# The Householder steps of a graph kernel: one TensorE visit per step instead of two, with the next row formed on VectorE

## The reference

```
h = relu(layernorm(x)); x = x + L0(h)   # normalised adj, two linear layers, each with a batch norm over all tokens
h = relu(layernorm(x)); x = x + L1(h)   # two products with adj, then LSTMs over windows of 1, 2, 3 and 4 nodes
h = relu(layernorm(x)); x = x + L2(h)   # U relu(U^T h W1 + b1) W2 + b2, U = eigenvectors of a Laplacian of adj
h = relu(layernorm(x)); x = x + L3(h)   # three graph convolutions with adj * adj
```

## Time and profile before

| | us |
|---|---|
| three runs, median (lowest to highest) | 1082.08 (1081.61 to 1082.16) |
| the profiled execution | 1077.69 |
| its span in the trace | 1075.9 |
| PE busy | 942.6 |
| DVE busy | 593.2 |
| ACT busy | 529.3 |
| POOL busy | 335.7 |

### The profile page before, as it was taken

How to read it: one execution, slowest core, us unless ns; L and a number is a source line. 1 busy time by engine, 2 the same in 40 slices (tenths; PEclk the granted TensorE clock), 3 DMA queues, 4 the chain that set the end, 5 groups by cost and what they waited for, 6 DMA issues and landing times.

```text
span 1075.9 us, 12192 instructions
## 1 busy us (share of the span) xinstructions
PE 942.6 (88%) x3721; PEld 573.0 (53%) x3721; DVE 593.2 (55%) x2897; ACT 529.3 (49%) x962; POOL 335.7 (31%) x404
## 2 busy tenths in 40 slices
PE   2787485589989999899898999995899999999998
PEld 1444232544546544456344553553675865866856
DVE  5899766767634785347999198965410501503101
ACT  1566364475453654536546365441646445445531
POOL 1333100036544265441665527653210200300000
PEclk9989798699999999999998999997799999999999
DMA  7000000000000000000000000000000100100101
GB/s 309 0 2 1 0 0 1 1 0 1 0 1 1 1 0 2 1 0 1 1 0 1 0 1 1 1 1 0 1 1 0 41 1 1 40 1 1 41 0 40
DMA packets 2961, 13.26 MB, mean 12 GB/s; under 512 B 464, under 2 KB 464, under 8 KB 2640
## 3 DMA queue, kind: packets, MB, share of 16 engines
q1 hardware_dynamic: 2896, 12.49, 2.9%
HBM read 8.30 MB, written 4.19 MB: 12 GB/s over the span
## 4 chain that ended last, share of the span: by engine, by line
PE 69%; DVE 19%; POOL 5%; ACT 4%; issue 2%; DMA 0%; SPq 0%; DVEq 0%; ACTq 0%; POOLq 0%
PE PS L384 68%; POOL BIG L846 4%; DVE ST L1354 2%; ACT T L750 2%; DVE T L1450 1%; DVE stats L1326 1%; ACT BIG L788 1%; DVE sc L1043 1%; DVE PS L1112 1%; ACT BIG L780 1%; DVE vcol L1040 1%; PE PS L541 1%; POOL sc L826 1%; DVE PS L1116 1%; DVE S L1061 1%
## 5 line engine op out<-in xcount | busy, mean ns | idle before, releaser
L384 PE MATMUL PS<-BIG,wts 128*128 128x512 f32 (+2 forms) x1264 | 520.8, 569 | 19.2 <-ACT BIG L780 10.0
L384 PEld LDWEIGHTS PS<-BIG,wts 128*128 128x128 f32 x1264 | 243.5, 198 | 255.1 <-issue 206.6
L846 POOL TENSOR_TENSOR BIG<-BIG 128x256 f32<-128x256 f32 (+2 forms) x272 | 257.4, 950 | 299.6 <-ACT BIG L780 239.1
L780 ACT ACTIVATE BIG<-PS,lbias 128x256 f32<-128x256 f32 (+2 forms) x312 | 170.6, 561 | 172.5 <-PE PS L384 171.5
L688 ACT ACTIVATE BIG<-PS 128x1024 f32<-128x1024 f32 x64 | 65.5, 1023 | 88.5 <-PE PS L384 88.5
L1465 DVE TENSOR_TENSOR X<-X,PS 128x512 f32<-128x512 f32 x64 | 43.4, 682 | 118.5 <-PE PS L384 87.1
L696 ACT ACTIVATE T<-X,shift,rstd 128x128 f32<-128x128 f32 x192 | 78.4, 482 | 52.4 <-DVE shift L1342 52.4
L688 ACT ACTIVATE T<-PS 128x512 f32<-128x512 f32 x96 | 55.3, 593 | 98.1 <-PE PS L384 98.1
L384 PE MATMUL PS<-T,wts 128*128 128x512 f32 x192 | 99.4, 648 | 1.1 <-ACT T L688 0.8
L1486 DVE TENSOR_TENSOR T<-PS,wts 128x512 f32<-128x512 f32 x16 | 11.1, 691 | 150.9 <-PE PS L384 150.9
L834 POOL TENSOR_SCALAR rstd<-mv 128x4 f32<-128x4 f32 x48 | 10.9, 228 | 234.5 <-DVE mv L1333 234.5
(11 more groups left out here) (235 smaller groups left out, 1148.3 us busy)
## 6 DMA issues: line engine op xcount, KB each, us to landing
X<-x_in SPq DMA_DIRECT2D x1, 4096.0 KB, 12.5
out<-X SPq DMA_DIRECT2D x16, 256.0 KB, 2.0
wts<-w_in SPq DMA_DIRECT2D x1, 3605.5 KB, 21.3
cst<-cst_in SPq DMA_DIRECT2D x1, 371.0 KB, 3.3
AA<-adj_in SPq DMA_DIRECT2D x2, 16.0 KB, 2.0
```

The source lines that it names most:

```text
L384: return nc.tensor.matmul(o, l, r, start=start, stop=stop)
L780: nc.scalar.activation(LB[:, q, {"i": I_, "g": G_, "f": F_, "o": O_}[g], 0:n], PS[:, 3 * q + rank[q] % 3, 0:n], ACT.Tanh if g == "g" else ...
L846: nc.gpsimd.tensor_tensor(out, a, b, op).then_inc(pool_set[q], 1)
```

## The change

The next row is not fetched from the updated S any more. With z = S v + kappa v, the update of S is S - (v z^T + z v^T)/(...), so row k+1 of the new S is the old row k+1 plus two multiples of v and z, which VectorE has as replicated rows. In each step:

- `row_product` is gone. `old_row` fetches row k+1 of S as it is before the update, as a product with a column of the identity, into eb(3). It is issued by `av_product`, just ahead of the product with vcol, behind the same wait on hh_v.
- VectorE forms kappa, the row z (`zrow`), its column value, and from these and eb(3) the next row `xrow`, in two `scalar_tensor_tensor`. The sums of squares and the column's own value (xc) are now three `tensor_tensor_reduce` on VectorE.
- The two rank-one updates of S (`update`) move out of the chain into the next step, where `aside` issues them with the two reductions, sign and guard while the norm is computed.
- `need(n)` waits for the operation number n, where `sync` waited for all or all but one.
- From step 31 on a second copy of the row and of z is kept in PSUM (two more instructions, and one more for the first element).
- The planner has one product pair per step, 5.4 of its clock apart (`PACE_AV`), where it had 1.8 and 4.9.

Counted per step in VectorE's order of the two kernels: in the first layer 16 instructions of the step before and 23 after, in the second layer 24 before and 34 after; one of them has an accumulator read before, four after. TensorE has two small products per step in both.

The diff, cut to its core:

```
-PACE_ROW = 1.8
-PACE_AV = 4.9
+PACE_AV = 5.4
...
+            def old_row(o, k):
+                n = NODES - 1 - k
+                return mm(o[:, 0:n], ident[0:NODES, k:k + 1].broadcast_to((NODES, P)), S[0:NODES, k + 1:NODES])
...
             def av_product(k):
                 pe.wait_ge(hh_v, k + 1)
+                if k + 1 < REFLECTIONS:
+                    old_row(eb(3), k + 1)
                 mm(eb(2)[:, 0:NODES - k], vcol[0:NODES, 0:1].broadcast_to((NODES, P)), S[0:NODES, k + 1:NODES + 1])\
                     .then_inc(hh_av, 1)
...
                 for k in range(lo, REFLECTIONS):
-                    yield PACE_ROW
-                    row_product(k)
                     yield PACE_AV
                     av_product(k)
...
-                row_product(r)
                 if n < L0_FIRST and is_chunk(n - 3):
                     w1(n - 3)
...
+            def update(k, in_psum):
+                trail = S[:, k + 1:NODES]
+                z = (eb(1) if in_psum else zrow)[:, 0:NODES - 1 - k]
+                first = op(v.scalar_tensor_tensor(trail, z, vn, trail, ALU.mult, ALU.add))
+                yield
+                dve.wait_ge(hh_ops, first)
+                op(v.scalar_tensor_tensor(trail, row_of(k, in_psum), zn, trail, ALU.mult, ALU.add))
+                yield
...
+                def aside():
+                    behind = update(k - 1, k > REFLECTED) if k else iter(())
+                    next(behind, None)
+                    rest = op(v.tensor_tensor_reduce(junks[:, 0, 0:m - 1], xr[:, 1:m], vr[:, 1:m], 1.0, 0.0, ALU.mult,
+                                                     ALU.add, r2))
+                    yield
+                    op(v.tensor_scalar(sg, x0, 0.0, 2.0, ALU.is_gt, ALU.mult))
+                    yield
+                    next(behind, None)
+                    yield
+                    op(v.tensor_tensor_reduce(junks[:, 1, 0:m], vr, ident[:, k + 1:NODES], 1.0, 0.0, ALU.mult, ALU.add, xc))
+                    yield
+                    dve.wait_ge(hh_ops, rest)
+                    op(v.tensor_scalar(guard, r2, TINY, 1e30, ALU.is_lt, ALU.mult))
+                    yield
+
+                off = aside()
+                squares = v.tensor_tensor_reduce(junks[:, 2, 0:m], xr, vr, 1.0, 0.0, ALU.mult, ALU.add, n2)
...
-                op(v.tensor_scalar(wcol[:, :], vcnn, eb(2)[:, m:m + 1], wp, ALU.mult, ALU.add))
-                op(v.scalar_tensor_tensor(trail, av, vcn, trail, ALU.mult, ALU.add))
-                sync()
-                v.scalar_tensor_tensor(trail, vr, wcol[:, :], trail, ALU.mult, ALU.add).then_inc(hh_S, 1)
+                dve.wait_ge(hh_v, k + 1)
+                need(hh[0])
+                need(op(v.tensor_scalar(kappa, eb(2)[:, m:m + 1], half_nc, None, ALU.mult)), beside)
+                got = op(v.scalar_tensor_tensor(zrow[:, 0:m], xr, kappa, eb(2)[:, 0:m], ALU.mult, ALU.add))
+                op(v.tensor_scalar(zc, vcol[:, :], kappa, S[:, NODES:NODES + 1], ALU.mult, ALU.add))
+                need(got, beside)
+                psum = k + 1 > REFLECTED
+                if k + 1 < REFLECTIONS:
+                    op(v.tensor_scalar(b0, zrow[:, 0:1], nc_, -1.0, ALU.mult, ALU.mult))
+                    got = op(v.scalar_tensor_tensor(eb(1)[:, NODES:NODES + m - 1], zrow[:, 1:m], a0, eb(3)[:, 0:m - 1],
+                                                    ALU.mult, ALU.add))
+                    if psum:
+                        op(v.scalar_tensor_tensor(eb(1)[:, 0:m], xr, kappa, eb(2)[:, 0:m], ALU.mult, ALU.add))
+                    need(got, beside)
+                    for p_ in range(2 if k + 1 >= REFLECTED else 1):
+                        got = op(v.scalar_tensor_tensor(row_of(k + 1, p_), xr[:, 1:m], b0, eb(1)[:, NODES:NODES + m - 1],
+                                                        ALU.mult, ALU.add))
+                    op(v.tensor_scalar(zn, zc, nc_, -1.0, ALU.mult, ALU.mult))
+                    need(got, beside)
```

More of the change, by code:

```diff
@@ L963, in _ @@
             step(v.tensor_copy(S[NODES:P, 0:NODES], ident[NODES:P, NODES:P]), "S")
-            v.sem_inc(hh_S, 1)
             norm, sg, hd, nc_, guard, m_, y_, beta = (s1(n) for n in (3, 4, 7, 8, 9, 11, 14, 5))
-            vcn, vcnn, wp = (s1(n) for n in (12, 13, 10))
+            xc, half_nc, kappa, vn, zc, zn, a0, b0 = (s1(n) for n in (12, 13, 10, 32, 33, 34, 35, 38))
             n2, r2 = s1(36), s1(37)
@@ L977, in op, with need @@
                 ins.then_inc(hh_ops, 1)
-            def sync_hh(back=0, beside=iter(())):
+                return hh[0]
+            def need(n, beside=iter(())):
                 next(beside, None)
                 beside_l1()
-                dve.wait_ge(hh_ops, hh[0] - back)
+                dve.wait_ge(hh_ops, n)
             I32 = mybir.dt.int32
@@ L1037, in reflection @@
-                sync()
-                op(v.tensor_scalar(beta, sg, -1.0, norm, ALU.add, ALU.mult))
-                sync()
-                op(v.tensor_scalar(vcol[:, :], C("next")[:, k:k + 1], beta, xm, ALU.mult, ALU.subtract))
-                op(v.tensor_scalar(v0, v0, beta, None, ALU.add))
-                sync()
-                op(v.tensor_scalar(hd, v0, beta, guard, ALU.mult, ALU.max))
-                v.tensor_tensor_reduce(junk[:, 0:m], trail, vr, 1.0, 0.0, ALU.mult, ALU.add, S[:, NODES:NODES + 1])\
-                    .then_inc(hh_v, 1)
@@ new lines, in reflection @@
+                need(op(v.tensor_scalar(beta, sg, -1.0, norm, ALU.add, ALU.mult)), beside)
+                op(v.tensor_scalar(vcol[:, :], C("next")[:, k:k + 1], beta, xc, ALU.mult, ALU.add))
+                if not by_pool:
+                    op(v.tensor_scalar(vr[:, 0:1], vr[:, 0:1], beta, None, ALU.add))
+                got = op(v.tensor_scalar(x0, x0, beta, None, ALU.add))
+                need(got, beside)
+                v.tensor_tensor_reduce(junks[:, 3, 0:m], trail, vr, 1.0, 0.0, ALU.mult, ALU.add, S[:, NODES:NODES + 1])\
+                    .then_inc(hh_v, 1)
@@ L1054, in reflection @@
+                need(op(v.tensor_scalar(hd, x0, beta, guard, ALU.mult, ALU.max)), beside)
+                need(op(v.reciprocal(nc_, hd)), beside)
+                op(v.tensor_scalar(half_nc, nc_, -0.5, None, ALU.mult))
+                op(v.tensor_scalar(a0, x0, nc_, -1.0, ALU.mult, ALU.mult))
+                op(v.tensor_scalar(vn, vcol[:, :], nc_, -1.0, ALU.mult, ALU.mult))
                 next(beside, None)
@@ L1508, in _ @@
                 add(ITER - 1, k, banks(k)[:, 1, :], D_PE.at(ITER - 1, "mix3"))
-PREP = {"BDA": 1, "BDAT": 2, "hat_rows": 11, "lap_rows": 18, "S": 24, "biases": 27, "diagonals": 29, "bound": 42,
-        "V": 96, "VT": 98, "U": 100, "AU": 103, "ritz": 108, "I+E": 121, "all": 127}
+PREP = {"BDA": 1, "BDAT": 2, "hat_rows": 11, "lap_rows": 18, "S": 23, "biases": 26, "diagonals": 28, "bound": 41,
+        "V": 95, "VT": 97, "U": 99, "AU": 102, "ritz": 107, "I+E": 120, "all": 126}
 def kernel(x, adj, **w):
```

94 lines of the change are left out of this document (42 added, 52 removed).

## The result

The changed kernel takes 1112.46 us as the median of four executions (1105.63 to 1254.03), of which one, 1254.03, was disturbed, so everything below goes by the other three, with a median of 1109.84. The kernel before takes 1082.07 (1081.61 to 1082.16). The ratio is 1.026, with an interval of 1.021 to 1.032. The forecast was 1102.8 with a range of 1084 to 1119: right in direction, and 7 us short of the 1109.84.

A forecast was written before the change was run, and what follows sets the result against it. VectorE instructions were taken to bound the first 186 us, time between TensorE's visits the next 550. Terms +15.6 + 2 + 5.5 + 6 + 0.5 - 8.9 = +20.7 on 1082.1 gave 1102.8 us, range 1084 to 1119.

The forecast's parts named there:

- Part 1: First layer, steps 0 to 30: VectorE's added instructions cost more than the removed meeting saves, +15.6 us, bounds +5 to +25.
- full step: First-layer step in which VectorE is filled with the layer's statistics; 12 of them, +1.05 us each, +12.6 in all.
- light one: First-layer step with only the two 512-column statistics beside it: 5.4 us against 4.69, four of them, +2.8.
- second half: First layer's later steps, where TensorE stood in the way: 5.4 us against 5.62 with one meeting, -3.0 in all.
- four had been given 3.2: First-layer steps before the statistics-filled ones, now waiting for two products in one visit after TensorE's pauses: +0.8 each, +3.2.
- the +2 for the clock: First layer: longer TensorE pauses bring more stretches at 1.2 GHz, about 1 us per step lost there; +2, 0 to 12.
- rival "faster": Added first-layer instructions slip into gaps between dependent ones and the second layer loses nothing: -4, 1078 us; chance 0.12.
- GpSimd's hold: Steps 0 to 30: VectorE's two-SBUF-input instructions wait for GpSimd's power, +8 to 16 on top, 1111 to 1119; chance 0.09.
- Part 2: Second layer: VectorE's late hh_v holds up TensorE's LSTM products; +5.5 in front parts, +6 beside 512-column LSTMs, +0.5.
- 2 x 3.5: Second layer's front parts, first two iterations: VectorE's step with four biases, 8.3 us, exceeds TensorE's work; +3.5 each.
- The term for the LSTMs: Second layer, layer norm or residual additions beside 512-column LSTMs: about 1 us in six to seven steps, +6, 0 to 12.
- Part 3: Third layer's entrance: the solver's end moves into the last LSTMs, so statistics follow the last residual addition; -8.9.

The follow-up runs named there:

- run 2: The changed kernel with 6.2 instead of 5.4 us of the planner's clock between column products in the second layer; 1093.9 us, ratio 1.011.
- run 7: The changed kernel with the new step in the first layer only, the old step and old paces in the second; 1098.96 us, ratio 1.019.
- run 9: Old step in first layer, new in second, 6.2 us per step, paces 44, 28, 47 before the three sums, 43 before the eigenvectors; 1064.17 us, ratio 0.985.
- run 10: The changed kernel, new step in both layers, paces 6.2 per step, 44, 28, 47 before the sums, 43 before the eigenvectors; 1083.3 us, ratio 1.004.
- run 1: The changed kernel with 46 instead of 38 us of the planner's clock before the bisection's first sum; 1103.95 us, ratio 1.021.
- run 8: The changed kernel with two more unused multiply-and-reduce instructions in each of steps 0 to 30; 1117.36 us, ratio 1.036.
- run 4: The changed kernel with the old step in the first layer, the new step in the second, at the changed kernel's paces; 1090.99 us, ratio 1.008.
- run 3: The kernel before with 33 instead of 38 us of the planner's clock before the second and third sums of the bisection; ratio 1.000.
- run 5: The kernel before with 38, 33 and 37 us of the planner's clock before its three sums and 42 before the eigenvectors; ratio 0.997.
- run 6: Old step in first layer, new in second, 6.2 us per step, 38, 33, 47 before the sums, 43 before the eigenvectors; 1071.11 us, ratio 0.992.

## Why the prediction was right, and where it was not

The stages of four runs, cut as in the table of before and after:

| stage (us) | run 2 | run 7 | run 9 | run 10 |
|---|---|---|---|---|
| first layer | 221.6 | 221.3 | 202.4 | 221.6 |
| pass 1 | 141.3 | 142.3 | 140.9 | 140.7 |
| pass 2 | 134.5 | 137.9 | 134.5 | 134.5 |
| pass 3 | 141.4 | 137.5 | 133.7 | 133.6 |
| pass 4 | 132.8 | 137.2 | 130.2 | 130.2 |

**Part 1: right, by its own steps.** The rows of after that answer show the new middle of a full step (VectorE's timeline):

```profile
75.65 0.22 DVE L1082 TENSOR_SCALAR sc<-PS,sc 128x1 f32<-128x1 f32 x1
75.91 0.27 DVE L1083 SCALAR_TENSOR_TENSOR zrow<-xrow,sc,PS 128x54 f32<-128x54 f32 x1
76.09 0.27 DVE L1084 TENSOR_SCALAR sc<-vcol,sc,S 128x1 f32<-128x1 f32 x1
76.28 0.20 DVE L1088 TENSOR_SCALAR sc<-zrow,sc 128x1 f32<-128x1 f32 x1
76.40 0.27 DVE L1089 SCALAR_TENSOR_TENSOR PS<-zrow,sc,PS 128x53 f32<-128x53 f32 x1
76.70 0.27 DVE L1095 SCALAR_TENSOR_TENSOR xrow<-xrow,sc,PS 128x53 f32<-128x53 f32 x1
...
77.01 0.21 DVE L1039 CUSTOM_DVE_ANT_0 junks<-xrow 128x53 f32<-128x53 f32 x1
77.14 0.08 DVE L1039 DVE_READ_ACCUMULATOR2_ANT sc<- 128x1 f32 x1
77.14 0.27 DVE L1009 SCALAR_TENSOR_TENSOR S<-zrow,sc,S 128x54 f32<-128x54 f32 x1
77.33 0.21 DVE L1025 CUSTOM_DVE_ANT_0 junks<-xrow 128x52 f32<-128x52 f32 x1
```

From kappa (75.65) to the first reduction (77.01) are 1.36 us, 0.12 of them the scaling of zc, so 1.24 where the sum had 1.42. A full step takes 6.21 to 6.31, one of them 6.52 (forecast 6.3), a light one 5.4 (5.4; one took 6.98), a step of the second half 5.38 (5.4). The column product of step 21 came 20.6 us late (19) and the second half gave back 3.2 (3.0). Within that, the six steps ahead of the full ones cost 6.6 where four had been given 3.2, and the light steps 4.3, so the +2 for the clock was not needed: five traces with the new step (after and runs 1, 2, 7 and 10) have between 58 and 76 us recorded at 1.2 GHz in the first layer and take 221.0 to 221.6 all the same. (The record of the clock begins only at its first rise, at 42 to 50 us; in after the 512-column products ahead of that start 0.85 us apart, as they do at 1.2 GHz.) Low clock costs there only once VectorE waits for the column product, as in run 8. That the added instructions could hide in gaps (rival "faster") is refuted by run 8, and that part 1 stands by itself is shown by runs 4 and 7.

**GpSimd's hold: does not decide.** In steps 0 to 31 the updates at L1012 that ran free of GpSimd's power took 0.249 us (26 of them), those beside it 0.257 (5); at L1009 30 beside it took 0.264, but these had all begun ahead of the power. The reductions at L1025, with two inputs in SBUF, are the better sign: 30 of them started while the power ran and took 0.205 us in the mean, where the reductions at L1039, all outside it, took 0.203. The rows of 0.20 us in the earlier trace rows were the right ones to follow.

**Part 2: near in total, by errors that cancel.** I set each LSTM product of after against its twin of the kernel before, both counted from the start of their pass. In pass 1 after is 5.3 us behind after 23 us, some 3 from 36 to 43 us, and then between 3.7 and 7.2; in pass 2 it is 4.7 behind after 25 us, and between 4.4 and 7.7 later. At their ends the passes are 5.7 and 4.5 behind. So the front parts cost 10.0 us in place of 2 x 3.5, and the layer norms and residuals beside LSTMs, to which I had given 6, cost nothing in the total. The step was sound (a step of VectorE does not fit into the front). The term for the LSTMs was not: there are six waits for a column product beside them, 5.3 us in all, but TensorE's other waits get shorter by part of it (for GpSimd at 36 us of pass 1 2.0 in place of 3.3, for ScalarE near the end of that pass 2.7 in place of 3.4). That pass 3 came out 1.8 us shorter than before, where I had 1.5, is luck: it has TensorE's wait of 7.6 us for the first sum in it, which I had not seen coming. In run 1, which asks for that sum later, it is 6.1 us shorter. Run 2 shows that the loss was one of pace: with 6.2 us per step the two passes together are 4.5 us shorter than before. Of the 5.7 us that pass 1 lost in after, up to 3 are not the change's: runs 1, 4 and 8 have the same instructions there and take 146.5, 145.0 and 145.7 us to its 148.1.

**Part 3: the step of the prediction that failed.** "The planner now puts all of this into the last LSTMs, so the statistics can follow the addition ... -8.9." The first half holds, in after too:

```profile
779.36 1.28 DVE L1508 TENSOR_TENSOR X<-X,PS 128x512 f32<-128x512 f32 x2 [0.96 <-PE PS L603]
780.56 0.86 DVE L1368 BATCH_NORM_STATS2 stats<-X 128x6 f32<-128x128 f32 x4
```

The statistics start with the end of the last residual, and the third layer's first product follows 6.6 us later (787.18), as forecast. But I took the earlier place of the solver's products for an earlier result. The planner's clock had moved them forward by 1.3 us per step, some 40 us by the end, since it counts TensorE's products and not VectorE's. VectorE, which got more to do per step, could not follow, and where TensorE had come late (13.70 us) it now came 9.0 early. The last residual ends 136.6 us after the start of the pass instead of 122.1: 9.1 for that wait with the transpositions and the clock behind it, 1.7 for the next three groups of small products, 2.2 for a later wait, and 1.5 for what else now stands inside the LSTM, less what it gains back. Runs 3 and 5 show the same on the old kernel: the gain of some 8 us exists, and it has a price inside the LSTM, for which my sum had nothing. The price hangs on the paces: 10.2 us in run 3, 5.6 in run 5, and only 1.6 in runs 9 and 10. There the last residual ends 123.7 us after the start of the pass, the statistics start with it, 7.0 us earlier than in the kernel before, and pass 4 takes 130.2 us instead of 137.2. Run 9 (the pass starts at 611.46):

```profile
733.87 1.29 DVE L1596 TENSOR_TENSOR X<-X,PS 128x512 f32<-128x512 f32 x2 [0.54 <-PE PS L616]
735.07 0.86 DVE L1454 BATCH_NORM_STATS2 stats<-X 128x6 f32<-128x128 f32 x4
```

So most of the -8.9 can be had, but only where nothing is asked for before it is there. With run 5's -2.6 in its place the forecast would have been 1109; that this is near the 1109.84 is no proof, since after itself had +5.9 in pass 4, and part 2 was 3.6 too high.

**The idea itself.** One meeting per step is worth having where TensorE is the bound: run 9 has it in the second layer alone, and of its 16.5 us below the kernel before, run 5, the old step with its solver's end moved, has some 3. The other 13 are the new step and its spacing together; the old step with other paces per step was not tried. In the first layer, where VectorE is the bound, it costs 18 to 19 us (runs 4, 7 and 10). After as a whole was slower for both reasons: 18 us for the first layer, and for the second a placement that asked for twelve column products, the first sum and the eigenvectors before their inputs were there.

What stays open: pass 3 takes 134.4 us in the kernel before and 137.5 in runs 5 and 7, which run the same instructions there (run 5 but for its last few). In the longer ones TensorE waits 5.7 us instead of 3.8 for a residual addition in the front part, and stays at 1.2 GHz for 6.8 us there instead of 3.4; why, no run tells. Pass 1 differs by up to 3 us in the same way, and there the low clock does not explain it: it has 16.7 us at 1.2 GHz in after (148.1 us long), 16.5 in run 1 (146.5), 17.5 in run 8 (145.7) and 13.5 in run 4 (145.0).

## What to carry to other kernels

Trading a meeting of two engines for instructions pays only on the side that has room: count the instructions against the engine that is bound in that stage, stage by stage, at their issue distance (here 0.13 us for a small independent VectorE instruction, 1.4 us for the new row). When a change alters how often a planner places something, it moves everything behind it; compare the new place of each later product with the time at which its input is ready in the old trace, since a transfer of idle time from the consumer to the bound engine turns slack into loss. And retune the placement before judging the change: here it was worth some 25 us, nearly all of what the change as first placed had cost.

## What the runs showed of the hardware

What a stop of TensorE costs beyond itself is less than half of the low stretch. In after, the granted clock went to 1.2 GHz 3 us into the stop of 9.04 us and back to 2.4 GHz 4.1 us after its end, 10.2 us in all. Since most of that lay in the stop, the LSTM products, of 336 columns, lost only some 0.7 us to it; I had expected 5. Behind stops of 5.3 to 7.6 us among products of 512 columns the loss was 1.8 us (after), 2.3 (run 6) and 2.4 (run 3).

GpSimd's LSTM products do hold up some VectorE instructions whose inputs are all in SBUF and wider than one element, and not only those with two tensors. The mask of the old step (L1006, 128x2) took 0.23 us in each of the 16 times it ran free in the second layer and 0.61 in the mean of the 14 beside such a product, up to 1.2. The solver's last multiplications are the same, here beside a GpSimd product from 690.14 to 691.41:

```profile
690.14 1.27 POOL L844 TENSOR_TENSOR BIG<-BIG 128x512 f32<-128x512 f32 x1 [0.64 <-ACT BIG L778]
...
690.18 1.31 DVE L1215 TENSOR_TENSOR Fq<-Fq,Trow 128x64 f32<-128x64 f32 x1
...
691.90 2.65 POOL L844 TENSOR_TENSOR BIG<-BIG 128x512 f32<-128x512 f32 x2 [0.49 <-ACT BIG L778]
...
692.08 0.55 DVE L1218 RECIPROCAL Fq<-Fq 128x64 f32<-128x64 f32 x1
```

Not all are held up: the reciprocal at 692.08, in SBUF and wholly beside a GpSimd product, took the 0.55 us of the free one at 689.59, and so did the layer's `bn_stats` of 128 columns (0.27 us beside in after's second layer, 0.28 free).

Every instruction of the new step that has a row in PSUM among its inputs takes the same time beside GpSimd and without it (at L1083 0.23 us in the 20 beside and 0.24 in the 11 free). For the LSTM products that agrees with the Trainium skill (GPSIMD Engine Reference, Specifications), which names VectorE instructions with two SBUF inputs, as the multiplication has, and those in a 2-port perf mode; in which mode the masks ran, with one tensor and one scalar, no row shows. The power beside steps 0 to 31 does not show it: the reductions at L1025 have two SBUF inputs and took 0.205 us beside it.
